# Two-layer perceiver block on one core: the first group's gate of the last feed-forward is computed inside the tail of the self attention before it

## The reference

```python
# _L1_attn_ref: weights are 4-bit codes times scales, 16 heads of 128
q = _mxfp4_matmul(x, wq_codes, wq_scales) + bq      # k and v alike
attn = jax.nn.softmax(scores, axis=-1)
return _mxfp4_matmul(out, wo_codes, wo_scales) + bo
# _L1_ffn_ref: 8 experts, top 2, all experts are computed for all tokens
probs = jax.nn.softmax(x @ gate_w, axis=-1)
gate_score, gate_idx = jax.lax.top_k(probs, TOP_K)
gate_score = gate_score / jnp.sum(gate_score, axis=-1, keepdims=True)
combine = jnp.einsum('tk,tke->te', gate_score, onehot) * alpha[None, :]
h = jax.nn.gelu(jnp.einsum('th,ehi->eti', x, fc1_w) + fc1_b[:, None, :], approximate=False)
y = jnp.einsum('eti,eih->eth', h, fc2_w) + fc2_b[:, None, :]
out = jnp.einsum('eth,te->th', y, combine)
```

## Time and profile before

| | |
|---|---|
| median of 3 runs | 2886.22 us (2885.09 to 2888.71) |
| profiled execution, its own time | 2886.39 us |
| its span | 2884.6 us |
| TensorE busy | 2734.6 us (95%) |
| VectorE, ScalarE, GpSimd busy | 1418.9, 1341.9, 680.7 us |
| mean granted TensorE clock | 0.978 |
| last self attention | from 2000.9 us to 2614.2 us of the span |
| last feed-forward | from 2616.0 us to the end |

### The profile page before, as it was taken

The page is one execution under the profiler, slowest core; times in us unless marked ns, Lnnn a source line. Parts: engine busy times, 40 slices in busy tenths (PEclk is TensorE's granted clock), DMA queues, the critical chain, the costliest instruction groups (busy, mean ns, idle before and its releaser), DMA issues. The chain is left out here.

```text
span 2884.6 us, 49670 instructions
## 1 busy us (share of the span) xinstructions
PE 2734.6 (95%) x13964; PEld 2084.2 (72%) x13964; DVE 1418.9 (49%) x4720; ACT 1341.9 (47%) x4875; POOL 680.7 (24%) x867
## 2 busy tenths in 40 slices
PE   6999999979899999987999999997999999997999
PEld 5888888868544444445677777776788888876887
DVE  3555555467577744444655555544233333333343
ACT  2555555446566666653555444444322222221333
POOL 1333332146365500014333333211300000000000
PEclk8999999989999999999999999998999999998999
DMA  5222221020410034414544433334400000001000
GB/s 169 59 62 59 60 63 51 21 91 0 154 45 2 1 94 124 118 33 115 140 118 110 112 98 99 94 99 125 97 0 0 0 0 0 0 0 33 8 7 11
DMA packets 158156, 178.12 MB, mean 62 GB/s; under 512 B 31883, under 2 KB 125512, under 8 KB 157410
## 3 DMA queue, kind: packets, MB, share of 16 engines
q1 hardware_dynamic: 131730, 148.13, 17.4%
q0 software_dynamic: 13824, 25.23, 4.1%
q10 hardware_dynamic: 12496, 3.57, 0.8%
HBM read 141.12 MB, written 48.28 MB: 66 GB/s over the span
## 5 line engine op out<-in xcount | busy, mean ns | idle before, releaser
L221 PE MATMUL rt_kn_key_ps<-moe_w_wk,all_big 128*128 128x512 f32 x560 | 248.9, 598 | 0.8 <-DVE moe_kn_stats L270 0.4
L2136 PE MATMUL sa_work_ps<-sa_xnT,all_big 128*128 128x128 f32 x2048 | 235.9, 278 | 10.4 <-ACT sa_xnT L2206 5.8
L2136 PEld LDWEIGHTS sa_work_ps<-sa_xnT,all_big 128*128 128x128 f32 x2048 | 234.2, 195 | 11.2 <-ACT sa_xnT L2206 6.1
L528 PE MATMUL xa_misc_ps<-xa_xnT,cross_folded 128*128 128x256 f32 x1024 | 234.3, 383 | 6.2 <-ACT xa_squares L657 5.6
L681 ACT ACTIVATE xa_probsT<-xa_probsT_ps 128x256 f32<-128x256 f32 x512 | 191.4, 375 | 93.6 <-PE xa_probsT_ps L548 87.2
L571 PE MATMUL xa_misc_ps<-cross_folded,xa_mixT 128*128 128x256 f32 x1024 | 229.3, 379 | 0.0
L528 PEld LDWEIGHTS xa_misc_ps<-xa_xnT,cross_folded 128*128 128x128 f32 x1024 | 195.9, 192 | 40.1 <-ACT xa_squares L657 12.2
L571 PEld LDWEIGHTS xa_misc_ps<-cross_folded,xa_mixT 128*128 128x128 f32 x1024 | 194.6, 190 | 26.5
L221 PE MATMUL ex_kn_key_ps<-moe_w_wk,all_big 128*128 128x512 f32 x448 | 203.2, 597 | 0.7 <-DVE moe_kn_stats L270 0.7
L548 PE MATMUL xa_probsT_ps<-all_ident,xa_probs 128*128 128x128 f32 x1024 | 197.4, 275 | 4.7 <-DVE xa_probs L814 3.7
L814 DVE TENSOR_SCALAR xa_probs<-xa_probs,xa_share 128x257 f32<-128x257 f32 x512 | 184.3, 381 | 14.4 <-DVE xa_share L812 0.3
(11 more groups left out here) (310 smaller groups left out, 5270.7 us busy)
## 6 DMA issues: line engine op xcount, KB each, us to landing
all_big<-rk SPq DMA_DIRECT2D x256, 128.5 KB
xa_pair<-pairs SPq DMA_DIRECT2D x64, 256.5 KB, 14.9
pairs<-all_big SPq DMA_DIRECT2D x64, 128.5 KB, 2.9
xa_rows<-in_ctx_dram SPq DMA_DIRECT2D x64, 128.0 KB, 2.4
pairs<-xa_keys SPq DMA_DIRECT2D x64, 128.0 KB, 2.0
cross_folded<-in_L_ffn_w_gate_dram SPq DMA_DIRECT2D x32, 192.0 KB, 2.5
cross_folded<-in_L_ffn_w_up_dram SPq DMA_DIRECT2D x32, 192.0 KB, 2.7
xa_last_key<-in_ctx_dram SPq DMA_DIRECT2D x64, 64.0 KB, 3.0
```

The source lines that it names most:

```text
L221: pe.matmul(self.key_ps[m % self.banks][0:n, :], self.ctxT[:, c * P:c * P + n], self.wk[:, q * 512:(q + 1) * 512], start=True, stop=True). ...
L528: ins = pe.matmul(misc_ps[hp % 2][:, j * N:(j + 1) * N], folded[:, 2 * hp + j, c * P:(c + 1) * P], xnT[:, c, :], start=(c == 0), stop=(c = ...
L2136: ins = pe.matmul(ps[:, j, :], w[:, c, h * HD:(h + 1) * HD], xnT[:, c, :], start=(c == 0), stop=(c == NC - 1))
```

## The change

All that the feed-forward did for group 0 before its first expert product, except the bias product, is issued in the self attention, around its last tile. The buffers for it (`dense_tiles`) are now made beside the weights, ahead of the self attention, and handed to both parts as `f`; PSUM space is borrowed from the self attention (`turn_ps` and a bank of `score_ps`). It has 12 semaphores of its own, all of the self attention's scope, and the feed-forward has one fewer. In the feed-forward, the stages of group 0 are replaced by increments of the semaphores that they would have raised. The diff, without the moved buffer definitions and the rest of the moved body of `weigh`:

```diff
-def self_attention_fp4(nc, I, x_sb, ident, weights, ahead):
+def self_attention_fp4(nc, I, x_sb, ident, weights, ahead, w, f):
...
+        pair_set, f_var_ready, f_rstd_ready, f_normed, f_turned, f_xnT_ready = (sc.sem("f_" + n) for n in (
+            "pair_set", "var_ready", "rstd_ready", "normed", "turned", "xnT_ready"))
+        f_routed, f_shifted, f_exped, f_weighed, f_weight_turned, f_weightT_ready = (sc.sem("f_" + n) for n in (
+            "routed", "shifted", "exped", "weighed", "weight_turned", "weightT_ready"))
+        GT = 2
+        route_ps = score_ps[:, 0:G, :].rearrange("p h n -> p (h n)")
...
                 score(i + 1)
+            pe.wait_ge(f_normed, GT)
+            pe.wait_ge(xnT_ready, NT + 1)
+            for c in range(NC):
+                for t in range(GT):
+                    ins = pe.transpose(turn_ps[:, (c * GT + t) * P:(c * GT + t + 1) * P], f["xn"][:, t, c * P:(c + 1) * P], ident[:, :])
+            ins.then_inc(f_turned, 1)
+            pe.wait_ge(ahead_loaded, 16 * len(ahead))
+            pe.wait_ge(blocks_kept, NT * BT)
+            pe.wait_ge(f_xnT_ready, 1)
+            for t in range(GT):
+                for c in range(NC):
+                    ins = pe.matmul(route_ps[:, t * E1:(t + 1) * E1], f["xnT"][:, 0, c, t, :], w["gate_w"][:, c, :],
+                                    start=(c == 0), stop=(c == NC - 1))
+            ins.then_inc(f_routed, 1)
             mix(NT - 1, True)
             project_out(NT - 1)
+            pe.wait_ge(f_weighed, 1)
+            for t in range(GT):
+                ins = pe.transpose(route_ps[0:E1, D + t * P:D + (t + 1) * P], f["weight"][:, 0, t, :], ident[:, :])
+            ins.then_inc(f_weight_turned, 1)
...
             exp(NT - 1)
+            act.wait_ge(f_turned, 1)
+            act.activation(f["xnT"][:, 0, :, :, :], turn_ps[:, :].rearrange("p (c t n) -> p c t n", c=NC, t=GT), ACT.Copy
+                           ).then_inc(f_xnT_ready, 1)
+            act.wait_ge(f_shifted, 1)
+            act.activation(f["prob"][:, :, :], f["prob"][:, :, :], ACT.Exp).then_inc(f_exped, 1)
+            act.wait_ge(f_weight_turned, 1)
+            act.activation(f["weightT"][:, :, :], route_ps[0:E1, D:2 * D].rearrange("e (t n) -> e t n", t=GT), ACT.Copy
+                           ).then_inc(f_weightT_ready, 1)
...
             link = Chain(dve, dve_chain, (NT - 1) * LINKS + 2, passed)
+            dve.memset(f["pair"][:, :, :], -2.0).then_inc(pair_set, 1)
+            dve.wait_ge(added, NT - 1)
+            for t in range(GT):
+                link(dve.bn_stats(f["stats"][:, t, :], x_sb[:, t, :]), alone=True)
+                dve.bn_aggr(f["mv"][:, t, :], f["stats"][:, t, :]).then_inc(f_var_ready, 1)
+            dve.wait_ge(f_rstd_ready, 1)
+            for t in range(GT):
+                dve.tensor_scalar(f["xn"][:, t, :], x_sb[:, t, :], f["mv"][:, t, 0:1], f["rstd"][:, t:t + 1],
+                                  ALU.subtract, ALU.mult).then_inc(f_normed, 1)
             shift(NT - 1, link)
             divide(NT - 1, link)
             turn_probs(NT - 1)
+            dve.wait_ge(f_routed, 1)
+            logits = route_ps[:, 0:GT * E1].rearrange("q (t e) -> q t e", t=GT)
+            link(dve.tensor_reduce(f["top"][:, :], logits, AX_X, ALU.max))
+            dve.tensor_tensor(f["prob"][:, :, :], logits, per_tile(f["top"][:, :]), ALU.subtract).then_inc(f_shifted, 1)
             for g in range(NG):
                 keep_mix(NT - 1, g)
+            dve.wait_ge(f_exped, 1)
+            dve.wait_ge(pair_set, 1)
+            dense_weights_of(dve, f, w["alpha"], f["weight"][:, 0, :, :], link).then_inc(f_weighed, 1)
             add(NT - 1, link)
...
             with pool.Fori(0, NT - 1) as i:
                 scale_of(i + 2)
+            link = Chain(pool, pool_chain, NT + 1, passed)
+            pool.wait_ge(f_var_ready, GT)
+            apart(pool, passed)
+            link(pool.tensor_scalar(f["rstd"][:, :], f["mv"][:, :, 1], LN_EPS, None, ALU.add))
+            pool.tensor_tensor(f["rstd"][:, :], f["rstd"][:, :], minus_half[:, :].broadcast_to([P, GT]), ALU.pow
+                               ).then_inc(f_rstd_ready, 1)
...
+def dense_weights_of(dve, f, alpha, weight, link):
+
+    TOP = 2
+    prob, top, total, best, pair, rest = (f[n] for n in ("prob", "top", "total", "best", "pair", "rest"))
+    link(dve.tensor_reduce(total[:, :], prob[:, :, :], AX_X, ALU.add))
...
+    return dve.tensor_tensor(weight, rest[:, :, :], alpha[:, :].unsqueeze(1).broadcast_to([P, 2, E1]), ALU.mult)
...
-            for stage in prepare.values():
-                stage(0, 0)
+            pe.sem_inc(x_turned, 1)
+            pe.sem_inc(routed, 1)
+            pe.sem_inc(weight_turned, 1)
+            bias(0, 0)
+            pe.wait_ge(xnT_ready, 1)
             first(0, 0, 0)
             pe.wait_ge(fc2_loaded, 16)
...
-            for stage in prepare.values():
-                stage(0, 0)
+            act.sem_inc(xnT_ready, 1)
+            act.sem_inc(exped, 1)
+            act.sem_inc(weightT_ready, 1)
...
-            dve.memset(pair[:, :, :], -2.0).then_inc(pair_set, 1)
-            dve.wait_ge(pair_set, 1)
-            link = Chain(dve, dve_chain, 0, passed)
-            for stage in prepare.values():
-                stage(0, 0, link)
-            assert link.n == LINKS, link.n
+            dve.sem_inc(var_ready, GT)
+            dve.sem_inc(normed, GT)
+            dve.sem_inc(shifted, 1)
+            dve.sem_inc(weighed, 1)
+            dve.sem_inc(dve_chain, LINKS)
...
-            scale_of(0)
+            pool.sem_inc(rstd_ready, 1)
+            pool.sem_inc(pool_chain, 1)
             with pool.Fori(0, GROUPS) as g:
                 scale_of(g + 1)
```

More of the change, by code:

```diff
@@ L2385, in dense_experts @@
         ITERS = GROUPS // U
-        TOP = 2
-        W = 8
         STEPS = E1
@@ L2392, in dense_experts @@
         fc1_b, fc2_b, gate_w, alpha = w["fc1_b"], w["fc2_b"], w["gate_w"], w["alpha"]
[L2393 to L2398, removed]
+        minus_half = sc.sb("minus_half", [P, 1])
+        stats, mv, rstd, xn, xnT, prob, top, weight, weightT = (f[n] for n in (
+            "stats", "mv", "rstd", "xn", "xnT", "prob", "top", "weight", "weightT"))
         hidden = sc.sb("hidden", [P, 2, FC, GT * P])
@@ L2405, in dense_experts @@
         fc2_loaded = sc.sem("fc2_loaded")
-        pair_set, half_set = sc.sem("pair_set"), sc.sem("half_set")
+        half_set = sc.sem("half_set")
         passed, dve_chain, pool_chain = sc.sem("passed"), sc.sem("dve_chain"), sc.sem("pool_chain")
@@ L2553, in normalize @@
                                       ALU.subtract, ALU.mult).then_inc(normed, 1)
-            def per_tile(x, n):
-                return x.unsqueeze(2).broadcast_to([P, GT, n])
             def shift(g, p, link):
@@ L2561, in shift @@
                 link(dve.tensor_reduce(top[:, :], logits, AX_X, ALU.max))
-                dve.tensor_tensor(prob[:, :, :], logits, per_tile(top[:, :], E1), ALU.subtract).then_inc(shifted, 1)
+                dve.tensor_tensor(prob[:, :, :], logits, per_tile(top[:, :]), ALU.subtract).then_inc(shifted, 1)
             def weigh(g, p, link):
                 dve.wait_ge(exped, g + 1)
[L2566 to L2578, removed]
-                link(dve.reciprocal(total[:, :], total[:, :]))
-                link(dve.tensor_tensor(rest[:, :, :], rest[:, :, :], per_tile(total[:, :], E1), ALU.mult))
-                dve.tensor_tensor(weight[:, p, :, :], rest[:, :, :], alpha[:, :].unsqueeze(1).broadcast_to([P, GT, E1]), ALU.mult
-                                  ).then_inc(weighed, 1)
+                dense_weights_of(dve, f, alpha, weight[:, p, :, :], link).then_inc(weighed, 1)
             prepare = {0: stats_of, 1: normalize, 4: shift, 5: weigh}
@@ L2659, in build @@
                             sa1)
-        w, loads = dense_weights(nc, Scope(nc, ctx, "ff1"), I)
-        self_attention_fp4(nc, I, x_sb, ident, sa1, loads)
-        dense_experts(nc, I, x_sb, ident, out, w)
+        dense = Scope(nc, ctx, "ff1")
+        w, loads = dense_weights(nc, dense, I)
+        f = dense_tiles(dense)
+        self_attention_fp4(nc, I, x_sb, ident, sa1, loads, w, f)
+        dense_experts(nc, I, x_sb, ident, out, w, f)
 OUT_SHAPE = (B, T, D)
```

24 lines of the change are left out of this document (23 added, 1 removed).

## The result

| | before | after |
|---|---|---|
| median, 20 runs each | 2889.51 us (2884.91 to 2891.28) | 2882.94 us (2879.03 to 2887.03) |
| ratio, 95% interval | | 0.9978 (0.9972 to 0.9984) |
| profiled execution, its span | 2886.39, 2884.6 us | 2885.56, 2883.8 us |
| end of the second cross attention | 1998.6 us | 2003.4 us |
| from there to the end | 886.0 us | 880.4 us |

The change makes the kernel 0.22% faster, 6.4 us by the ratio (4.6 to 8.1). 7.0 us were forecast, but the predicted time of 2879.3 us lies 3.6 us too low, and the range missed the measured median. The base was the larger error: three runs before had a median of 2886.22, twenty have 2889.51.

The account below looks back on a forecast made before the run. TensorE was taken to bound the kernel, apart from stage hand-overs. Gain 7.7 us less 0.65 for clears gave 7.0; 2886.39 - 7.0 = 2879.4, with the three-run median 0.17 lower 2879.3 us, range 2876.3 to 2881.9.

Parts of the forecast that it names:

- The base: Whole kernel before the change: profiled execution of 2886.39 us, median of three runs 0.17 lower; the gain was subtracted from it.
- What was covered: Group 0's work moved around the self attention's last tile: claimed to fit in existing waits, normalisation with 1.9 us to spare.
- the rival that ends slower: Self attention's last tile: mix stuck behind the gate products on in-order TensorE, 2892 us or more; chance 3%.
- The tail: After the last output projection: two weight turns and ScalarE's copy added before the block ends, +0.2 us, bounds 0 and 0.5.
- the saved clear: Between blocks: the feed-forward has one semaphore fewer for SyncE to clear, giving 0.05 us.
- The clears: Before the self attention: 12 more semaphores cleared by SyncE while all engines wait, +0.65 us, bounds 0 and 0.8.
- The load took the chain's place: Feed-forward start: fc2's load, landing 8.0 us after issue, makes TensorE pause 5.2 us; some 5 of 11.8 us not won.
- the load is hidden: Rival in the feed-forward: fc2 does not hold TensorE, gain 15.5 us less 0.65, time 2871.5 us; chance 3%.
- The estimate of 6.8 us: fc2's 2 MB load by the skill's formula, about 2.0 us plus bytes over 436 GB/s; forecast used the trace's 8.0.
- The clock: TensorE in the feed-forward: falls to half speed in the 5.2 us pause for fc2, costing 2.4 us, likely 1.5 to 2.8.
- the bound of 3.7: Feed-forward: at most 3.7 us lost to TensorE's half-speed clock after the pause for fc2.
- The rival with the high clock throughout: Feed-forward: fc2 holds TensorE but the clock stays high, gain 9.4 us, time 2876.8 us; chance 10%.

Follow-up runs that it names:

- Both experiments on the load: Changed kernel with fc2 loaded ahead in the self attention, without its wait: ratio 0.9964 to before; changed kernel with fc2 loaded twice in sequence: 2888.7 us, one run.
- fc2 ahead: Changed kernel with the fc2 load issued in the self attention and no wait for it in the feed-forward: 2878.9 us, ratio 0.9964 to the kernel before.

## Why the prediction was right or wrong

**The base was wrong.** The step that failed is "The median of the three runs is 0.17 lower, so 2879.3 us": it took three runs and one profile as the kernel's level, and let the range hold hardly more than the bounds of the gain. Twenty runs put the level 3.3 us higher, single runs 6 us apart, and the later session 29 us. The gain, forecast 7.0, was 6.4 (4.6 to 8.1); 7.0 taken from 2889.51 would have given 2882.5, against 2882.94 measured. That the gain came so near is in part luck, since single terms of it were off, as follows.

**What was covered was covered.** Normalisation before the scores, gate products before the mix, weights under the projection: each where forecast. Counted from the end of the last scores, turn and gate products started within 0.1 us of the forecast; weights and output bias ended 3.0 us after the last kept mix, 3.5 forecast. The mix was not delayed, and the rival that ends slower found nothing. The tail was lengthened by 0.03 us (last projection's end to the barrier, 2.33 after 2.30), against 0.15 forecast with the saved clear.

**The clears**: 2.92 us from the cross attention to the block after 2.26, +0.66, forecast 0.65.

**The load took the chain's place.** Landing 8.3 us after issue (8.0 forecast), second expert's products 8.6 us after the barrier (8.2 by the forecast's 2616.2 and 2624.4). The bias product came 0.7 us after it instead of 0.3, held by ScalarE's increments; beneath the load that cost nothing. Both experiments on the load confirm it as the cause; "the load is hidden" has fallen. The estimate of 6.8 us by the Trainium skill's page "DMA: Bandwidth & Descriptors" (Anatomy of one DMA), whose fit is for GpSimd's path, would have been too short for this load, issued by SyncE: it took 8.0 to 8.3 us in every trace that issues it in the feed-forward.

**The clock: right sign, wrong place, size somewhat low.** A pause of 5.2 us was forecast, in which the clock would fall. The pause was 2.52 us, because the clock fell before it, at 2623.07, 3.2 us after the last weight turn's end and just behind the block change's pause of 2.81 us. The forecast had bias and first expert at the high clock there; they took 5.4 us instead of 2.6, beneath the load and so at no cost. The full clock came 6.1 us after work resumed: 3.1 us lost, 2.4 forecast, inside the bound of 3.7. The rival with the high clock throughout has fallen. By what the Trainium skill's page "TensorE: Matmul & The Clock Gate" (HAM oscillation) says of DMA waits, the burst behind the wait starts at the low clock. It did in this trace, and where other products filled the wait, the second expert's ran at 1.00; but the fall itself came ahead of the wait, not in it.

**The sum by stretches**, from the two profiles: clears +0.7; the self attention from its barrier to its last mix +1.3 (TensorE waited 2.19 us instead of 0.94 for GpSimd's scaling, which had waited for scales that DMA brought); the last mix -0.75 (5.72 us after 6.47, its low clock ended sooner); tail 0; feed-forward -6.8 (forecast -7.7, the tail's 0.15 included: the clock took 0.7 more than forecast, the second expert's start came 0.4 later). Together -5.6, as measured. The second and third vary from execution to execution without the change: over all traces, the stretch up to the mix was 598.1 to 599.6 us in kernels with the change and 598.2 to 599.9 in those without, the mix 5.4 to 6.7 and 5.6 to 6.5.

## What to carry to other kernels

When a chain in front of a stage is taken away, look at what the stage itself only then starts: here a load of 8 us, unseen under a chain of 12, became the wait. Moving the load as well took another 4.8 us off the stage, beside the first 6.8, while moving the chain's last third was worth nothing as long as the load stayed. Count a pause on TensorE with the low clock behind it; here even block changes of 2.8 and 1.3 us were followed by it. And for an absolute time take the level from many runs: a gain worked out from one trace can be right to a microsecond while the base under it moves by several.

## What was not expected of the hardware

With fc2 ahead, a pause of 2.78 us (the clock 1.00 up to 2619.6, 0.50 after) and even one of 1.31 us were followed by the low clock, 6.8 and 3.4 us long; the pauses read beforehand were of 3.7 us and more. Useless products made the feed-forward's stretch 2.7 us shorter. And the unaltered kernel ran 2884.9 to 2891.3 us in one session and 2911.9 to 2921.7 in the last one; between two profiles 26.5 of 31 us lay in the routing ahead of the experts and the gathering ahead of the second cross attention.
